# A decoder layer's expert lookup: first-table matmuls in 64-column tiles, and the one-hots built token by token on VectorE

## The chip, the cores and the metric

The kernel runs on one core of a Trainium2 chip. The metric is the device time of one execution in microseconds (us); lower is better. Kernels are compared by the median of several executions.

The engines that matter here are TensorE (PE in the profile; its weight loads are PEld), VectorE (DVE), ScalarE (ACT), GpSimd (POOL) and SyncE (SP), which starts the transfers. Each has its own instruction stream, and they meet only at semaphores.

## The reference, cut to what matters

A decoder layer in three parts: a single-head linear attention with a causal mask, a dynamic-time-warping alignment against a context, and a product-key expert layer. The change lies in the third:

```python
# x: 32*256 rows of 256; 8 heads, 8 experts of 16384 a head and row; fp32 throughout
sim = einsum('pbnhd,hkpd->pbnhk', q, keys_p)          # 2 x 64 scores a head
scores, idx = top_k(sim, 8)                           # the best 8 of each half
all_scores = scores[0][..., :, None] + scores[1][..., None, :]
sc, pk = top_k(all_scores, 8)                         # the best 8 pairs
indices = take(idx[0] * 64 + idx[1], pk)
wd = down[indices]
hmid = sigmoid(sc) * gelu(einsum('bnd,bnhkd->bnhk', inputs, wd))
out = einsum('bnhk,bnhkd->bnd', hmid, up[indices])
x = layernorm(x + out)
```

An index is at most 64*63 + 63 = 4095, so only the first 4096 rows of `down` and `up` are reached.

## The kernel before, in words

Nothing is gathered. The kernel computes all 4096 hidden values of every row with the first table (`dnT`, transposed), applies gelu, multiplies by a coefficient that is the gate where an expert was chosen and zero elsewhere, and multiplies by the second table (`up`).

The coefficients of a row are an outer product summed over its 64 picks: expert = 32 * p + c, with p (0 to 127) in `valsT[:, :, 0]`, c (0 to 31) in `valsT[:, :, 1]`, and the gate in `valsT[:, :, 2]`. The partition of these is the pick (64 picks of a row of each of the group's two tiles, 128 together), the column is the token. For each token there are two one-hots: `hot_hi` (128 picks by 128 values of p) and `hot_lo` (128 picks by 64: 32 values of c for each of the two tiles, times the gate). TensorE multiplies them, `hot_hi` as the stationary operand in two halves of 64 columns.

The third part works on 32 groups of 256 rows. A group has 16 steps (NQ = 16), each of 8 tokens (TQ = 8; a column of `valsT` serves a row of both tiles) and 2 of the 32 values of c. The order is written out by hand, and each engine runs one loop over groups: the first two and the last two groups are peeled, and a loop of two groups a pass does the rest.

- VectorE in a step q: `hots` for step q + 3 (AHEAD = 3; four buffers of one-hots, so it waits for the matmuls of step q - 1), then `coefs` of step q, which multiplies the coefficients in PSUM into `gelh`. `norm` of the group before comes in step 0, `scale` in step 6. After the 16 steps it runs `route` twice (top 8, pairs, indices) for the group two ahead.
- GpSimd in a step: one multiply of `hot_lo` by the gate, after VectorE's `hot_ready`; it signals `gated_ready`.
- TensorE in a step: `coefs` (wait for `gated_ready` and for the PSUM bank of two steps ago; 16 matmuls of 64 columns), then `hidden` of the next group (4 matmuls of 128 stationary columns and 256 moving ones; PSUM banks in turn, freed by gelu). `turn_vals` (transposes of the picks) comes in step 10, `turn` in step 15. After the steps: `score` for tile 0, half an `output` of 32 matmuls, `score` for tile 1, and the other 48 `output` matmuls.
- ScalarE: gelu of each `hidden` result, the gates' sigmoid, the copies of transposes.

In the profile each fp32 matmul is two records of TensorE: the 16 of `coefs` are 32, the 4 of `hidden` are 8.

Of the kernel before, what the change touches and what calls it, by code (L numbers as in the profile page):

```python
# [15 lines left out]
ALU = mybir.AluOpType  # L16
# [3 lines left out]
P = 128  # L20
# [5 lines left out]
def decoder_layer(nc, x, xT, ctx_rows_d, ctx_cols_d, wqkvT_d, bqkv_d, projT_d, projb_d, gamma_d, beta_d, wq_d,  # L26
# [4 lines left out]
    CC = C // P  # L31
# [14 lines left out]
    with ctx:  # L46
        def sb(name, shape, dt=F32):
            return ctx.enter_context(nc.sbuf_tensor(name, shape, dt))

        def sem(name):  # L50
            return ctx.enter_context(nc.semaphore(name))
# [12 lines left out]
        iota = sb("iota", [P, T])  # L64
# [81 lines left out]
        pool_rests, dve_rests, act_rests = sem("pool_rests"), sem("dve_rests"), sem("act_rests")  # L146
# [15 lines left out]
        gate_ready = sem("gate_ready")  # L162
        valsT_mm = sem("valsT_mm")
        valsT_ready = sem("valsT_ready")
        hot_ready = sem("hot_ready")
        gated_ready = sem("gated_ready")
        a_mm = sem("a_mm")
        coef_ready = sem("coef_ready")
# [13 lines left out]
        def rest(eng, spare):  # L182

            eng.sem_inc(spare, 1)

        def later(b, n):

            return not (isinstance(b, int) and b < n)
# [28 lines left out]
        with ExitStack() as st:  # L217
# [33 lines left out]
            block = st.enter_context(nc.Block())  # L251
# [295 lines left out]
        with ExitStack() as st:  # L547
# [32 lines left out]
            block = st.enter_context(nc.Block())  # L580
# [267 lines left out]
        with ExitStack() as st:  # L848
            def se(name, shape, dt=F32):
                return st.enter_context(nc.sbuf_tensor(name, shape, dt))  # L850
# [3 lines left out]
            NQ = 16  # L854
            TQ = P // NQ
            CL = 32
            BUFS = 4
            dnT = se("dnT", [P, CC, CL, P])
            up = se("up", [P, CL, C])
            gelh = se("gelh", [P, 2, CL, 2, P])  # L860
            hot_hi = se("hot_hi", [P, BUFS, TQ, P])
            hot_lo = se("hot_lo", [P, BUFS, TQ, 2 * CL])
            offs = se("offs", [P, 2 * CL])
            x2_res = se("x2_res", [P, 2, 2, C])
            x2T = se("x2T", [P, CC, 2, P])
# [11 lines left out]
            valsT = se("valsT", [P, 2, 3, P])  # L877
# [9 lines left out]
            ps_h = [bank[3 + i][:, :].rearrange("p (c n) -> p c n", c=2) for i in range(2)]  # L887
# [8 lines left out]
            def groups(eng, step):  # L896

                for g in range(2):
                    step(g, g)
                with eng.Fori(1, GROUPS // 2 - 1) as j:  # L900
                    for par in range(2):
                        step(2 * j + par, par)
                for g in range(GROUPS - 2, GROUPS):
                    step(g, g % 2)
# [5 lines left out]
            block = st.enter_context(nc.Block())  # L910
# [34 lines left out]
                for par in range(2):  # L945
                    sp.wait_ge(y_out[par], 16 * GROUPS // 2)

            @block.gpsimd
            def _(pool):
                def gated(g, par, q):  # L950

                    pool.wait_ge(hot_ready, g * NQ + (q + 1))
                    rest(pool, pool_rests)
                    pool.tensor_tensor(hot_lo[:, q % BUFS], hot_lo[:, q % BUFS],  # L954
                                       valsT[:, par, 2, TQ * q:TQ * (q + 1), None].to_broadcast([P, TQ, 2 * CL]),
                                       ALU.mult).then_inc(gated_ready, 1)

                def step(g, par):
                    for q in range(NQ):
                        gated(g, par, q)  # L960
                groups(pool, step)

            @block.tensor
            def _(pe):
                def turn(g, par):
# [29 lines left out]
                def hidden(g, q):  # L995

                    pe.wait_ge(x2T_ready, g + 1)
                    if later(g, 1) or q >= 2:
                        pe.wait_ge(gel_ready, g * NQ + (q - 1))
                    for c in range(2):  # L1000
                        for k in range(CC):
                            mm = pe.matmul(ps_h[q % 2][:, c, :], dnT[:, k, 2 * q + c, :],  # L1002
                                           x2T[:, k, :, :].rearrange("p a t -> p (a t)"),
                                           start=(k == 0), stop=(k == CC - 1))
                    mm.then_inc(h_mm, 1)

                def coefs(g, q):
# [24 lines left out]
                for q in range(NQ):  # L1032
# [4 lines left out]
                    for k in range(CC):  # L1037
                        for c in range(2):
                            mm = pe.transpose(ps_dn[q % 4][:, k, c, :], dn[:, 2 * q + c, k * P:(k + 1) * P], ident[:, :])
# [3 lines left out]
                for q in range(NQ):  # L1043
                    hidden(0, q)
# [101 lines left out]
            def _(dve):  # L1146
# [52 lines left out]
                def hots(g, par, q):  # L1199

                    if q == 0:
                        dve.wait_ge(valsT_ready, g + 1)
                    if later(g, 1) or q >= BUFS:
                        dve.wait_ge(a_mm, g * NQ + (q + 1 - BUFS))
                    rest(dve, dve_rests)
                    some = slice(TQ * q, TQ * (q + 1))
                    dve.tensor_tensor(hot_hi[:, q % BUFS], iota[:, None, 0:P].to_broadcast([P, TQ, P]),  # L1207
                                      valsT[:, par, 0, some, None].to_broadcast([P, TQ, P]), ALU.is_equal)
                    dve.tensor_tensor(hot_lo[:, q % BUFS], offs[:, None, :].to_broadcast([P, TQ, 2 * CL]),  # L1209
                                      valsT[:, par, 1, some, None].to_broadcast([P, TQ, 2 * CL]), ALU.is_equal)\  # L1210
                        .then_inc(hot_ready, 1)

                def coefs(g, par, q):

# [37 lines left out]
                for q in range(AHEAD):  # L1252
                    hots(0, 0, q)
# [63 lines left out]
```

## Time and profile before

| | |
|---|---|
| Median of 3 runs | 3309.46 us (3308.94 to 3311.43) |
| The profiled execution's own time | 3312.22 us |
| Its span in the profile | 3310.5 us |
| PE busy | 3016.2 us (91%), 26660 instructions |
| DVE busy | 2774.3 us (84%), 8246 instructions |
| ACT busy | 736.2 us (22%) |
| POOL busy | 597.7 us (18%), of which 536.1 in the gate multiply |

Busy time says who works, not who is waited for: the chain of waits does that. Durations of neighbouring VectorE instructions overlap by some tens of ns, so what a further instruction costs is read from the distance between two starts, called spacing below, and not from its duration alone. The third part begins at about 590 us of the span; the first one-hot is written at 620.83 us.

### The profile page before, as it was taken

What the parts mean: (1) busy time and instruction counts of PE and PEld (TensorE: products, weight loads), DVE (VectorE), ACT (ScalarE), POOL (GpSimd) and SP (SyncE); (2) the same over time, 40 slices, a digit from 0 to 9 for tenths busy, and PEclk for the clock granted to TensorE, in tenths of its full rate; (3) what the DMA queues carried; (4) which work ended last, traced back from release to release, by engine and by line L of the source; (5) the groups of instructions that cost most, each with busy time, mean ns of one, the idle gap of its engine ahead of it and who ended that gap; (6) DMA issues with size and microseconds to landing.
All of it is one profiled execution on the core that took longest, in us unless ns stands there. A gap on an engine that the chain in (4) does not pass through costs nothing.

```text
span 3310.5 us, 73159 instructions
## 1 busy us (share of the span) xinstructions
PE 3016.2 (91%) x26660; PEld 2388.6 (72%) x26660; DVE 2774.3 (84%) x8246; ACT 736.2 (22%) x1302; POOL 597.7 (18%) x599
## 2 busy tenths in 40 slices
PE   8981047699999999999999999999999999999997
PEld 4651035588888888888888888888888888888886
DVE  5557977798889898989898988888888888888865
ACT  3540024212222222222222222222222222222210
POOL 1230000022222121212122222222222222222221
PEclk9985555899999999999999999999999999999997
DMA  5441025200000000000000000000000000000000
GB/s 154 140 132 46 0 73 172 73 1 11 11 11 11 11 11 11 11 11 11 11 11 11 11 11 11 11 12 11 12 11 12 11 11 11 11 11 11 8 8 7
DMA packets 88552, 93.42 MB, mean 28 GB/s; under 512 B 6109, under 2 KB 86910, under 8 KB 88062
## 3 DMA queue, kind: packets, MB, share of 16 engines
q1 hardware_dynamic: 88206, 88.74, 8.6%
q8 instruction: 225, 3.69, 0.4%
q14 instruction: 121, 0.99, 0.1%
HBM read 60.94 MB, written 27.79 MB: 27 GB/s over the span
## 4 chain that ended last, share of the span: by engine, by line
PE 80%; DVE 2%; issue 0%; ACT 0%; DVEq 0%; ACTq 0%
PE bank L1002 29%; PE bank L1025 27%; PE bank L1015 16%; PE bank L982 7%; PE bank L973 1%; DVE hot_hi L1207 1%; PE bank L992 0%; ACT dnT L1117 0%; DVE top_i L1157 0%; DVE gelh L1220 0%; DVE hot_lo L1209 0%; DVE top L1153 0%; DVE sel_i L1171 0%; DVE sel L1167 0%; DVEq L1238 0%
## 5 line engine op out<-in xcount | busy, mean ns | idle before, releaser
L1002 PE MATMUL bank<-x2T,dnT 128*128 128x256 f32 x4096 | 1011.8, 390 | 0.4 <-ACT gelh L1104 0.4
L954 POOL TENSOR_TENSOR hot_lo<-hot_lo,valsT 128x512 f32<-128x512 f32 x512 | 536.1, 1047 | 2492.5 <-DVE hot_lo L1209 2492.5
L1207 DVE TENSOR_TENSOR hot_hi<-iota,valsT 128x1024 f32<-128x1024 f32 x512 | 858.7, 1677 | 52.2 <-issue 36.7
L1025 PE MATMUL bank<-up,gelh 128*128 128x256 f32 x4096 | 896.6, 380 | 0.9 <-DVE gelh L1220 0.9
L1025 PEld LDWEIGHTS bank<-up,gelh 128*128 128x128 f32 x4096 | 779.8, 190 | 133.1 <-issue 28.7
L1002 PEld LDWEIGHTS bank<-x2T,dnT 128*128 128x128 f32 x4096 | 738.1, 190 | 111.2 <-issue 1.3
L1015 PEld LDWEIGHTS bank<-hot_lo,hot_hi 128*64 128x64 f32 x16384 | 529.5, 140 | 195.7 <-issue 178.5
L1015 PE MATMUL bank<-hot_lo,hot_hi 128*64 128x64 f32 x16384 | 600.2, 227 | 28.2 <-DVE gelh L1220 27.6
L1104 ACT ACTIVATE gelh<-bank 128x512 f32<-128x512 f32 x512 | 305.7, 597 | 938.6 <-PE bank L1002 937.9
L1220 DVE TENSOR_TENSOR gelh<-bank,gelh 128x512 f32<-128x512 f32 x512 | 347.6, 679 | 52.4 <-PE bank L1015 49.6
L1209 DVE TENSOR_TENSOR hot_lo<-offs,valsT 128x512 f32<-128x512 f32 x512 | 349.5, 683 | 0.0
L1153 DVE MAX8 top<-bank 128x8 f32<-128x64 f32 x1024 | 140.8, 216 | 145.0 <-PE bank L982 144.8
L982 PE MATMUL bank<-keymap,xnT 128*128 128x512 f32 x512 | 237.6, 608 | 9.5 <-DVE top_i L1157 6.2
L1157 DVE FIND_INDEX8 top_i<-top,bank 128x8 uint32<-128x64 f32 x1024 | 205.1, 225 | 0.0
L982 PEld LDWEIGHTS bank<-keymap,xnT 128*128 128x128 f32 x512 | 99.6, 195 | 110.6 <-issue 103.2
L1104 ACT ACT_TABLE_LOAD x62 | 79.5, 1283 | 382.1 <-PE bank L1002 382.1
L677 PE MATMUL bank<-fold,lo_hi 128*80 128x32 f32 x4 | 0.7, 326 | 178.0 <-DVEq L780 178.0
L677 PEld LDWEIGHTS bank<-fold,lo_hi 128*80 128x80 f32 x4 | 0.6, 242 | 178.2 <-DVEq L780 178.2
L1093 ACT ACTIVATE vals<-sel 128x64 f32<-128x64 f32 x64 | 16.5, 257 | 413.0 <-DVE sel L1167 412.7
L1093 ACT ACT_TABLE_LOAD x32 | 41.1, 1283 | 298.6 <-DVE sel L1167 298.6
L1171 DVE FIND_INDEX8 sel_i<-sel,pair 128x8 uint32<-128x64 f32 x512 | 101.1, 220 | 0.0
L1179 DVE TENSOR_TENSOR pick<-half_i,iota 128x512 f32<-128x512 uint32 x128 | 82.8, 689 | 4.8
(140 smaller groups left out, 1994.2 us busy)
## 6 DMA issues: line engine op xcount, KB each, us to landing
x_scratch<-x_sb SPq DMA_DIRECT2D x64, 256.0 KB, 2.2
xT_sb<-in_xT SPq DMA_DIRECT2D x32, 256.0 KB, 2.7
x_sb<-in_x SPq DMA_DIRECT2D x32, 256.0 KB, 2.8
x_again<-x_scratch SPq DMA_DIRECT2D x32, 256.0 KB, 2.6
x_tile<-x_scratch SPq DMA_DIRECT2D x32, 256.0 KB, 3.0
x_res<-x_scratch SPq DMA_DIRECT2D x32, 256.0 KB, 2.8
out_y<-yo SPq DMA_DIRECT2D x32, 256.0 KB, 2.2
gelh<-in_table SPq DMA_DIRECT2D x4, 1024.0 KB, 8.9
```

What stands on the lines that cost most here:

```text
L954: pool.tensor_tensor(hot_lo[:, q % BUFS], hot_lo[:, q % BUFS], valsT[:, par, 2, TQ * q:TQ * (q + 1), None].to_broadcast([P, TQ, 2 * CL]), ...
L982: mm = pe.matmul(ps_score[p][:, :], xnT[:, k, a, :], keymap[:, k, p * NH * NK:(p + 1) * NH * NK], start=(k == 0), stop=(k == CC - 1))
L1002: mm = pe.matmul(ps_h[q % 2][:, c, :], dnT[:, k, 2 * q + c, :], x2T[:, k, :, :].rearrange("p a t -> p (a t)"), start=(k == 0), stop=(k == ...
L1015: mm = pe.matmul(ps_a[q % 2][rows, t * 2 * CL:(t + 1) * 2 * CL], hot_hi[:, q % BUFS, t, rows], hot_lo[:, q % BUFS, t, :], start=True, stop ...
L1025: mm = pe.matmul(ps_out[:, a, :], gelh[:, par, c, a, :], up[:, c, :], start=(c == 0), stop=(c == CL - 1))
L1104: act.activation(gelh[:, par, 2 * q:2 * q + 2, :, :].rearrange("p c a t -> p c (a t)"), ps_h[q % 2], ACT.Gelu).then_inc(gel_ready, 1)
L1153: dve.max(out=top[:, p, h, :], in_=ps_score[p][:, h * NK:(h + 1) * NK])
L1157: last = dve.max_index(out=top_i[:, p, h, :], in_max=top[:, p, h, :], in_values=ps_score[p][:, h * NK:(h + 1) * NK])
L1171: dve.max_index(out=sel_i[:, h, :], in_max=sel[:, h, :], in_values=pair[:, h, :, :].rearrange("p a b -> p (a b)"))
L1207: dve.tensor_tensor(hot_hi[:, q % BUFS], iota[:, None, 0:P].to_broadcast([P, TQ, P]), valsT[:, par, 0, some, None].to_broadcast([P, TQ, P] ...
L1209: dve.tensor_tensor(hot_lo[:, q % BUFS], offs[:, None, :].to_broadcast([P, TQ, 2 * CL]), valsT[:, par, 1, some, None].to_broadcast([P, TQ, ...
L1220: dve.tensor_tensor(some, ps_a[q % 2][:, :].rearrange("p (t a c) -> p c a t", t=TQ, a=2), some, ALU.mult)\
```

## The change

The first-table matmuls of `hidden` are split: instead of 4 matmuls of 128 stationary columns there are 8 of 64, which write the lower and the upper 64 partitions of the same PSUM tile in turn. The moving operand stays the whole 256 columns, so each is streamed twice.

The one-hots of a step are no longer two VectorE instructions over 8 tokens and one on GpSimd. They are 16 VectorE instructions, two a token, with the token's value as a per-partition scalar operand: one compares `iota` with p, the other compares `offs` with c and multiplies by the gate. GpSimd does nothing in the third part, and VectorE signals `gated_ready` itself.

```diff
@@ GpSimd
-            @block.gpsimd
-            def _(pool):
-                def gated(g, par, q):
-
-                    pool.wait_ge(hot_ready, g * NQ + (q + 1))
-                    rest(pool, pool_rests)
-                    pool.tensor_tensor(hot_lo[:, q % BUFS], hot_lo[:, q % BUFS],
-                                       valsT[:, par, 2, TQ * q:TQ * (q + 1), None].to_broadcast([P, TQ, 2 * CL]),
-                                       ALU.mult).then_inc(gated_ready, 1)
...
@@ TensorE, hidden
-                            mm = pe.matmul(ps_h[q % 2][:, c, :], dnT[:, k, 2 * q + c, :],
-                                           x2T[:, k, :, :].rearrange("p a t -> p (a t)"),
-                                           start=(k == 0), stop=(k == CC - 1))
+                            for half in range(2):
+                                rows = slice(half * P // 2, (half + 1) * P // 2)
+                                mm = pe.matmul(ps_h[q % 2][rows, c, :], dnT[:, k, 2 * q + c, rows],
+                                               x2T[:, k, :, :].rearrange("p a t -> p (a t)"),
+                                               start=(k == 0), stop=(k == CC - 1))
@@ VectorE, hots
-                    some = slice(TQ * q, TQ * (q + 1))
-                    dve.tensor_tensor(hot_hi[:, q % BUFS], iota[:, None, 0:P].to_broadcast([P, TQ, P]),
-                                      valsT[:, par, 0, some, None].to_broadcast([P, TQ, P]), ALU.is_equal)
-                    dve.tensor_tensor(hot_lo[:, q % BUFS], offs[:, None, :].to_broadcast([P, TQ, 2 * CL]),
-                                      valsT[:, par, 1, some, None].to_broadcast([P, TQ, 2 * CL]), ALU.is_equal)\
-                        .then_inc(hot_ready, 1)
+                    for t in range(TQ):
+                        at = TQ * q + t
+                        dve.tensor_scalar(hot_hi[:, q % BUFS, t, :], iota[:, 0:P], valsT[:, par, 0, at:at + 1], None,
+                                          ALU.is_equal)
+                        last = dve.tensor_scalar(hot_lo[:, q % BUFS, t, :], offs[:, :], valsT[:, par, 1, at:at + 1],
+                                                 valsT[:, par, 2, at:at + 1], ALU.is_equal, ALU.mult)
+                    last.then_inc(gated_ready, 1)
```

VectorE's stream in two steps in the middle of a group, before the change. L1207 and L1209 write the one-hots of the step three ahead, L1220 multiplies the coefficients of this step into `gelh`.

```order
959 L1207 TENSOR_TENSOR hot_hi<-iota,valsT 128x1024 [waits a_mm]
960 L1209 TENSOR_TENSOR hot_lo<-offs,valsT 128x512
961 L1217 REGISTER_ALU
962 L1220 TENSOR_TENSOR gelh<-bank,gelh 128x64x8 [waits a_mm]
963 L1207 TENSOR_TENSOR hot_hi<-iota,valsT 128x1024 [waits a_mm]
```

The same place after it, where the lines are numbered lower since the GpSimd block is gone (L1194 and L1196 are the one-hots, L1207 is the multiply):

```order
1519 L1207 TENSOR_TENSOR gelh<-bank,gelh 128x64x8 [waits a_mm]
1520 L1194 TENSOR_SCALAR hot_hi<-iota,valsT 128x128 [waits a_mm]
1521 L1196 TENSOR_SCALAR hot_lo<-offs,valsT 128x64
1522 L1194 TENSOR_SCALAR hot_hi<-iota,valsT 128x128
1523 L1196 TENSOR_SCALAR hot_lo<-offs,valsT 128x64
...
1536 L1204 REGISTER_ALU
1537 L1207 TENSOR_TENSOR gelh<-bank,gelh 128x64x8 [waits a_mm]
```

A step of VectorE has gone from three instructions to 17; the waits stand where they stood. The total number of elements written is the same.

TensorE's stream in one step, before the change. L1015 is `coefs`, L1002 is `hidden`; a row's last number is its count.

```order
501 L1015 MATMUL bank<-hot_lo,hot_hi 64x64 [waits coef_ready,gated_ready]
502 L1015 MATMUL bank<-hot_lo,hot_hi 64x64 x15
504 L1002 MATMUL bank<-x2T,dnT 128x256 [waits gel_ready]
505 L1002 MATMUL bank<-x2T,dnT 128x256 x3
507 L1015 MATMUL bank<-hot_lo,hot_hi 64x64 [waits coef_ready,gated_ready]
```

And after it (L1001 is `coefs`, L988 is `hidden`):

```order
501 L1001 MATMUL bank<-hot_lo,hot_hi 64x64 [waits coef_ready,gated_ready]
502 L1001 MATMUL bank<-hot_lo,hot_hi 64x64 x15
503 L983 REGISTER_ALU [waits x2T_ready]
504 L988 MATMUL bank<-x2T,dnT 64x256 [waits gel_ready]
505 L988 MATMUL bank<-x2T,dnT 64x256 x7
```

Nothing is reordered; every matmul of a step now has 64 stationary columns. `gated_ready` is now raised by VectorE, directly behind its last one-hot.

## Rows read from the trace of the kernel before

**Rows 1.** The page's chain that ended last, by engine and line

```profile
PE 80%; DVE 2%; issue 0%; ACT 0%; DVEq 0%; ACTq 0%
```

**Rows 2.** Chain in order of time, one group: start us, us, what

```profile
1914.14 1.08 PE bank L1015 x32
1915.22 1.92 PE bank L1002 x8
...
1936.74 1.73 PE bank L1002 x8
...
1953.89 3.43 PE bank L982 x8
...
1967.66 20.72 PE bank L1025 x96
```

**Rows 3.** Timeline of ACT, line L1099: start us, us, what

```profile
690.19 0.48 ACT L1099 ACTIVATE valsT<-bank 128x384 f32<-128x384 f32 x1
...
3188.85 0.48 ACT L1099 ACTIVATE valsT<-bank 128x384 f32<-128x384 f32 x1
```

**Rows 4.** Timeline of DVE, end of route and first steps of a group

```profile
2040.73 2.20 DVE L1153 MAX8 top<-bank 128x8 f32<-128x64 f32 x16 [3.92 <-PE bank L982]
...
2069.79 1.22 DVE L1207 TENSOR_TENSOR hot_hi<-iota,valsT 128x1024 f32<-128x1024 f32 x1
...
2073.49 0.68 DVE L1226 TENSOR_TENSOR y<-bank,x_res 128x512 f32<-128x512 f32 x1
...
2075.26 1.23 DVE L1207 TENSOR_TENSOR hot_hi<-iota,valsT 128x1024 f32<-128x1024 f32 x1
2076.41 0.68 DVE L1209 TENSOR_TENSOR hot_lo<-offs,valsT 128x512 f32<-128x512 f32 x1
2077.01 0.68 DVE L1220 TENSOR_TENSOR gelh<-bank,gelh 128x512 f32<-128x512 f32 x1
2077.61 1.78 DVE L1207 TENSOR_TENSOR hot_hi<-iota,valsT 128x1024 f32<-128x1024 f32 x1
...
2080.52 1.86 DVE L1207 TENSOR_TENSOR hot_hi<-iota,valsT 128x1024 f32<-128x1024 f32 x1
```

**Rows 5.** Timeline of DVE and POOL in mid-group

```profile
2009.72 1.04 POOL L954 TENSOR_TENSOR hot_lo<-hot_lo,valsT 128x512 f32<-128x512 f32 x1 [1.86 <-DVE hot_lo L1209]
2010.06 0.15 DVE L1237 RECIPROCAL rs<-sd 128x2 f32<-128x2 f32 x1
2010.29 0.94 DVE L1242 TENSOR_SCALAR yo<-y,mv,rs 128x256 f32<-128x256 f32 x2
2011.15 1.21 DVE L1207 TENSOR_TENSOR hot_hi<-iota,valsT 128x1024 f32<-128x1024 f32 x1
```

**Rows 6.** L516, two per-partition scalars: duration minimum/median/maximum; one pair, timeline

```profile
L516 DVE TENSOR_SCALAR x_sb<-y,mv,rs x64: 389/404/1182, 48.1 to 229.8; 128x256 f32<-128x256 f32 x64
...
201.98 0.72 DVE L516 TENSOR_SCALAR x_sb<-y,mv,rs 128x256 f32<-128x256 f32 x2
```

**Rows 7.** Groups by line and form (busy us, mean ns): copies and casts

```profile
L536 DVE CAST iota<-iota_i 128x256 f32<-128x256 int32 x1 | 0.3, 271 | 0.0
L537 DVE CAST iota<-iota_i 128x8 f32<-128x8 int32 x1 | 0.2, 152 | 0.0
```

**Rows 8.** Timeline of DVE, small instructions with an immediate or one scalar

```profile
2049.99 0.20 DVE L1175 TENSOR_SCALAR half_i<-sel_i 128x64 uint32<-128x64 uint32 x1
2050.11 0.19 DVE L1176 TENSOR_SCALAR half_i<-sel_i 128x64 uint32<-128x64 uint32 x1
...
519.63 0.48 DVE L789 SCALAR_TENSOR_TENSOR mask<-iota,bounds,ramp 77x256 f32<-77x256 f32 x1 [0.33 <-issue]
520.03 0.15 DVE L814 SCALAR_TENSOR_TENSOR nb<-mv,rs 128x2 f32<-128x2 f32 x1
```

**Rows 9.** Waits over the span: us in total, times, longest us

```profile
DVE hot_hi L1207 <- issue: 36.7, 13, 3.0
```

**Rows 10.** Windows: us, busy (x) by engine, PEclk, DMA share, GB/s

```profile
120.00:230.00 110.00, 107.27 (x514) 68.70 (x513) 62.26 (x204) 60.10 (x155) 33.74 (x39) 0.92 0.41 133
```

More of the change, by code:

```diff
@@ L164, in decoder_layer @@
         valsT_ready = sem("valsT_ready")
-        hot_ready = sem("hot_ready")
         gated_ready = sem("gated_ready")
@@ L946, in _ @@
                     sp.wait_ge(y_out[par], 16 * GROUPS // 2)
-            @block.gpsimd
-            def _(pool):
-                def gated(g, par, q):
-                    pool.wait_ge(hot_ready, g * NQ + (q + 1))
-                    rest(pool, pool_rests)
-                    pool.tensor_tensor(hot_lo[:, q % BUFS], hot_lo[:, q % BUFS],
-                                       valsT[:, par, 2, TQ * q:TQ * (q + 1), None].to_broadcast([P, TQ, 2 * CL]),
-                                       ALU.mult).then_inc(gated_ready, 1)
[L958 to L961, printed above, removed]
             @block.tensor
```

## The prediction

> **What bounds the kernel now.** I read the chain of waits first, then the timelines of single engines. The chain puts 80% of the span on TensorE [rows 1]. In order of time it is TensorE alone [rows 2]: a step is 1.08 us of coefficient matmuls (L1015) and 1.92 us of first-table matmuls (L1002), 3.0 us, with no wait. Behind the 16 steps come scores and the second table, from 1953.89 to 1988.38. The copy of `valsT` comes once a group: its first and last starts are 30 groups apart, (3188.85 - 690.19)/30 = 83.29 us a group [rows 3]. TensorE sets this period.
>
> VectorE is close behind. It starts a `hot_hi` every 2.91 us in mid-group (2077.61 to 2080.52), waits 3.92 us for the scores once a group, and otherwise hardly stops [rows 4]. So it has 0.1 us of slack a step. The question is whether its new step still fits beside TensorE's.
>
> **What VectorE gives back.** Undisturbed, `hot_hi` occupies 1.15 us (start 2075.26, next start 2076.41), `hot_lo` 0.60 and the multiply 0.60: 2.35 us. Nearly every later `hot_hi` lasts 1.78 us [rows 4], since GpSimd's multiply of 1.04 us runs beside its start. That pause goes with the GpSimd work: 2.91 would be 2.35 if nothing else changed.
>
> **What VectorE's 16 new instructions cost.** 8 tokens, each with one 128-column compare (one scalar read per partition) and one 64-column compare and multiply (two such scalars). The trace has neither, so I build them from spacing, start to start.
> - Per column: `hot_hi` against `hot_lo`, (1.15 - 0.60)/512 = 1.07 ns with two tensor inputs. A cast of 256 columns against one of 8: (271 - 152)/248 = 0.48 ns with one tensor input [rows 7]. So one-input instructions from SBUF run two columns at a time.
> - Fixed: L1175 to L1176, 64 columns and an immediate, is 0.12 us [rows 8]. Less 64 x 0.5 that is 85 ns.
> - Per-partition scalars: L516 has exactly two, over 256 columns. A pair lasts 0.72 us, one 0.404, so the second starts 0.32 us after the first [rows 6]. Less 130 for the columns and 85 fixed, two scalars cost 105 ns, some 52 each. L789, with one scalar and two tensors, is followed after 0.40 us [rows 8]; 256 x 1.07 and the 60 ns that `hot_lo` takes above its columns make 0.33, which leaves 70 ns for one scalar.
>
> Does L516 really run two columns at a time, with dear scalars, or one, with free ones? Columns at 1.07 ns would be 274 of its 320 ns, so the spacing alone allows both. The same form in L1242 decides it for me: its pair grows from 0.72 to 0.94 us when a GpSimd multiply runs beside it [rows 5], as `hot_hi` grows. The Trainium skill, "SBUF — State Buffer", says that a one-input VectorE instruction is held off by GpSimd only in a two-port mode. By that rule the 0.94 speaks for two columns at a time; no run so far shows the mode itself.
>
> So the 128-column compare is 64 + 85 + 55 = 204 ns, and the 64-column one 32 + 85 + 105 = 222 ns: 426 ns a token, 3.41 us a step. With the multiply's 0.60 the step is **4.01 us**, against 2.91 now and against TensorE's 3.0. Bounds from the nearest rows: with free scalars and columns at full price it is L516's 320 ns less 128 and less 192 columns at 1.07, 183 + 115 = 298 ns a token, giving a step of 2.98; with full price for both, 524 ns, giving 4.8. I take 426, which rests on the one form with two scalars. Break-even: VectorE's period equals 83.29 when the step is 3.14 us, or 317 ns a token.
>
> **What TensorE saves, and why it doesn't count.** Each first-table matmul becomes two on different halves of the array. A 256-column record takes 1.73/8 = 216 ns, so a 64-column one alone would take 54; the 32 of L1015 take 1.08 us, 34 ns each [rows 2], so halves do run side by side. Behind the transposes the 8 records of L1002 take 1.73 us instead of 1.92 [rows 2]: 0.19 us is lost at the switch from 64-column to 128-column matmuls. The Trainium skill, "TensorEngine Tiling (Array Packing)", section Tiling Modes, says that changing the tiling mode drains TensorE; the 0.19 agrees. With one mode throughout I expect 2.8 us a step, at most 2.6 if `coefs` gains as well. This lies under VectorE's 4.0 us and is worth nothing. The one place without one-hots, `hidden` of group 0, keeps its 1.73.
>
> **The new period.** VectorE per group: 16 x 4.01 = 64.2; two routes 2040.73 to 2069.79 = 29.06; `norm` 2073.49 to 2075.26 = 1.77 [rows 4]; `scale` 2010.06 to 2011.15 less the GpSimd pause of 0.22 = 0.87 [rows 5]. Sum 95.9. No wait is left in it. The scores of tile 0 need step 15 of TensorE, which may run as soon as VectorE has finished step 13, so they are done before the route and the 3.92 us goes. The second table takes 1953.89 + 3.43 to 1967.66 + 20.72 = 31.1 us with the score inside [rows 2], while VectorE runs routes and a set of one-hots, 29.1 + 3.4 = 32.5: just covered. VectorE's waits for code at the loop's start, 36.7 us in 13 [rows 9], were in TensorE's shadow and now count.
>
> Sum against the span of 3310.5: 30 x (95.9 - 83.29) = 378, and 37 for the loop's start. The first three sets take 10.2 us from 620.83, 2 us beyond the score that follows. Eleven steps of group 0 before the first `valsT` mark, 11 x (4.01 - 2.91) = 12. Five steps of group 30 behind the last mark, 5 x (4.01 - 3.0) = 5. In the last group 12 steps write one-hots, 12 x 1.10 = 13. Total +447, a span of 3757. The profiled execution's own time is 1.7 above its span and 2.8 above the median, so the median would be **3756 us**, 13.5% slower.
>
> **The rivals.**
> - *A, on the other side: scalars cost nothing, columns full price.* For it: L516's 0.32 us, and L1175's 0.12, fit as well. Against: L1242 beside GpSimd, and 70 ns for L789's scalar. A VectorE step of 2.98 makes its group 47.7 + 31.7 and 1.2 for the loop, 80.6; TensorE's with 0.19 saved a step is 80.25. So about 80.6, 30 x 2.7 = 81 less and some back at the ends: 3235.
> - *B, on the other side too: two columns at a time and scalars hidden behind the instruction before.* 149 + 117 = 266 ns a token, step 2.73, under TensorE's 2.81. Then TensorE stays the bound and its 0.19 a step counts: 31 x 16 x 0.19 = 94, so 3215. It decides from 276 ns a token down; between 276 and 317 VectorE sets the pace and is still faster than before. Against it: L516's pair would be spaced 215 ns and is 320. The Trainium skill, "VectorE: DVE Perf Modes", section on the TRN2 errata, gives 58 cycles and half a cycle a column here: as an estimate 127 + 94 = 221 ns a token. By that rule B holds; the trace's two-scalar row speaks against it.
> - *C: the halves do not run side by side over 256 columns.* `hidden` would take 16 x 216 = 3.45 us, a step 4.53, a group 107.8: +24.5 x 31 and 28 for group 0's `hidden`, 4100. Against it: the 34 ns.
> - *D: dearer scalars or full-price columns besides.* 474 to 524 ns a token: +48 to +98 x 4096 tokens = 200 to 400 more, 3950 to 4150.
> - *E: TensorE, idle a third of the time, is granted less clock.* At 1.2 GHz its step would be 5.6 us and set the pace. Against it: at 0.92 mean in the first part [rows 10], where it has small work with gaps. It would be busy without a pause as soon as it slowed. Some 100 us on top of the forecast if it happens in part.
>
> **How the numbers follow.** Forecast 0.70, A 0.10, B 0.05, C 0.03, D 0.08, E 0.04. Each 10 ns a token is 41 us; the forecast's own range is +-25 ns, 3655 to 3860. A range with eight chances in ten takes some of D and E and ends at 3930, and on the low side 3600. What can be told from no change is 0.2%, 7 us. Faster: A and B, 0.15. Same: a token within a few ns of 317, 0.02. Slower: the rest, 0.83.
>
> **What the profile after would show.** VectorE busy in nearly every slice, and most of the chain on the two one-hot lines; `valsT` starts 97 us apart; a token's two instructions spaced 0.43 us, the 64-column one no cheaper than the 128-column one; TensorE waiting for VectorE's `hot_lo` about 1.2 us a step; L988's 16 records in 1.7 us. I am wrong if a token takes under 317 ns, or if L988's records are spaced 216 ns.

## The result, and the profile after

The changed kernel takes **3739.29 us** (median of 4, 3735.7 to 4032.77) against 3309.52 (3308.94 to 3311.43) for the kernel before: a ratio of **1.129** [1.127, 1.132]. The forecast was 3756, slower. One of the four runs, the one of 4032.77 us, had a granted clock of 0.749 against 0.927 to 0.930 in the others; it is left out of the ratio, and no profile shows why it was slow. The profiled execution took 3740.94 us with a span of 3739.2, 428.7 longer than that of before.

The page after: busy time by engine, then VectorE in 40 slices, the chain by engine and by line, and the groups that answer to the changed lines.

```profile
PE 2999.6 (80%) x30756; PEld 2259.9 (60%) x30756; DVE 3349.2 (90%) x15414; ACT 735.7 (20%) x1302; POOL 61.5 (2%) x87
...
DVE  4557786999999999999999999999999999999975
...
DVE 57%; PE 19%; issue 6%; DVEq 3%; ACT 0%; ACTq 0%
DVE hot_lo L1196 21%; DVE hot_hi L1194 19%; PE bank L1011 14%; DVE gelh L1207 8%; DVE top_i L1143 2%; PE bank L1001 2%; PE bank L966 2%; DVE top L1139 1%; DVE sel_i L1157 1%; PE bank L988 1%; DVE sel L1153 1%; DVEq L1214 1%; DVE pick L1165 0%; DVE pick L1170 0%; DVE half_key L1173 0%
...
L1196 DVE TENSOR_SCALAR hot_lo<-offs,valsT 128x64 f32<-128x64 f32 x4096 | 1251.4, 306 | 0.0
L1194 DVE TENSOR_SCALAR hot_hi<-iota,valsT 128x128 f32<-128x128 f32 x4096 | 1132.6, 277 | 52.8 <-issue 36.9
L1001 PE MATMUL bank<-hot_lo,hot_hi 128*64 128x64 f32 x16384 | 603.7, 228 | 445.0 <-DVE gelh L1207 443.8
...
L1139 DVE MAX8 top<-bank 128x8 f32<-128x64 f32 x1024 | 140.0, 211 | 8.2 <-PE bank L966 8.2
```

The chain has turned over: 80% on TensorE [rows 1] is now 57% on VectorE, most of it on the two one-hot lines. VectorE is at 9 from the eighth slice to the last but two. TensorE's busy time is nearly unchanged, but `coefs` (L1001) now sits idle behind VectorE for 444 us. The route's wait for scores, 3.92 us in the group of [rows 4] and 144.8 us in the whole run before, is down to a single wait of 8.2 us (L1139).

VectorE's timeline after, one step of mid-group, against [rows 4]:

```profile
2047.13 0.68 DVE L1207 TENSOR_TENSOR gelh<-bank,gelh 128x512 f32<-128x512 f32 x1
2047.73 0.28 DVE L1194 TENSOR_SCALAR hot_hi<-iota,valsT 128x128 f32<-128x128 f32 x1
2047.93 0.31 DVE L1196 TENSOR_SCALAR hot_lo<-offs,valsT 128x64 f32<-128x64 f32 x1
2048.15 0.28 DVE L1194 TENSOR_SCALAR hot_hi<-iota,valsT 128x128 f32<-128x128 f32 x1
...
2051.08 0.68 DVE L1207 TENSOR_TENSOR gelh<-bank,gelh 128x512 f32<-128x512 f32 x1
```

A token is 0.42 us (2047.73 to 2048.15), a step 3.95 (2047.13 to 2051.08), with no wait in it. Note that the durations, 0.28 and 0.31, would make 0.59 a token: neighbours overlap, and only the spacing adds up.

The copies of `valsT` after, against [rows 3]; the first and last are 30 groups apart:

```profile
704.82 0.49 ACT L1085 ACTIVATE valsT<-bank 128x384 f32<-128x384 f32 x1
...
1954.41 0.48 ACT L1085 ACTIVATE valsT<-bank 128x384 f32<-128x384 f32 x1
...
2052.47 0.49 ACT L1085 ACTIVATE valsT<-bank 128x384 f32<-128x384 f32 x1
...
2147.73 0.48 ACT L1085 ACTIVATE valsT<-bank 128x384 f32<-128x384 f32 x1
...
3592.37 0.49 ACT L1085 ACTIVATE valsT<-bank 128x384 f32<-128x384 f32 x1
```

(3592.37 - 704.82)/30 = 96.25 us a group, 83.29 before. These two groups take 98.06 and 95.26 us. The loop holds two groups, and in every second one VectorE waits some 2.8 us at the loop's start (the 36.9 us of L1194, in 13 waits; the profile names nothing that it waited for). Over the run the groups with that wait take 97.05 to 98.06 us and the others about 95.2, so 1.8 to 2.8 us of it shows in the period.

TensorE after, behind the second table of one group, where finished one-hots wait for it; then the first step that VectorE holds up:

```profile
2106.77 1.15 PE L1001 MATMUL bank<-hot_lo,hot_hi 128*64 128x64 f32 x32
2107.76 1.90 PE L988 MATMUL bank<-x2T,dnT 128*64 128x256 f32 x16
2109.49 1.10 PE L1001 MATMUL bank<-hot_lo,hot_hi 128*64 128x64 f32 x32
2110.42 1.90 PE L988 MATMUL bank<-x2T,dnT 128*64 128x256 f32 x16
...
2118.61 1.15 PE L1001 MATMUL bank<-hot_lo,hot_hi 128*64 128x64 f32 x32 [0.98 <-DVE gelh L1207]
```

The 16 records of L988 take 1.73 us (2107.76 to 2109.49), 108 ns each where a whole one of 128 columns takes 216 (1.73/8 in [rows 2]): the halves run side by side. `coefs` takes 0.93 (2109.49 to 2110.42), so an unhindered step is 2.66 us, where [rows 2] had 1.08 + 1.92 = 3.0. TensorE got faster and waits.

Is it the narrower form that is faster, or that the form no longer changes? The last step of a group before the change tells. There the whole matmuls of `hidden` stand between transposes and scores, which have 128 stationary columns too:

```profile
2035.26 1.89 PE L1002 MATMUL bank<-x2T,dnT 128*128 128x256 f32 x8
2036.99 3.60 PE L982 MATMUL bank<-keymap,xnT 128*128 128x512 f32 x8
```

They take 1.73 us (2035.26 to 2036.99), just as long as the halves. So the narrow form is no faster in itself; what was saved lay at the changes between 64 and 128 columns.

### The profile page after: what moved, and what is told of

Read it like the earlier page. It is cut to its first block, busy times and chain, and to the rows that moved or that the text cites. A ratio compares the mean times of both kernels' runs of the same rounds, so it can differ in the third digit from the quotient of the medians.

```text
span 3739.2 us, 87018 instructions
## 1 busy us (share of the span) xinstructions
PE 2999.6 (80%) x30756; PEld 2259.9 (60%) x30756; DVE 3349.2 (90%) x15414; ACT 735.7 (20%) x1302; POOL 61.5 (2%) x87
## 4 chain that ended last, share of the span: by engine, by line
DVE 57%; PE 19%; issue 6%; DVEq 3%; ACT 0%; ACTq 0%
DVE hot_lo L1196 21%; DVE hot_hi L1194 19%; PE bank L1011 14%; DVE gelh L1207 8%; DVE top_i L1143 2%; PE bank L1001 2%; PE bank L966 2%; DVE top L1139 1%; DVE sel_i L1157 1%; PE bank L988 1%; DVE sel L1153 1%; DVEq L1214 1%; DVE pick L1165 0%; DVE pick L1170 0%; DVE half_key L1173 0%
## 5 line engine op out<-in xcount | busy, mean ns | idle before, releaser
L1196 DVE TENSOR_SCALAR hot_lo<-offs,valsT 128x64 f32<-128x64 f32 x4096 | 1251.4, 306 | 0.0
L1194 DVE TENSOR_SCALAR hot_hi<-iota,valsT 128x128 f32<-128x128 f32 x4096 | 1132.6, 277 | 52.8 <-issue 36.9
L988 PE MATMUL bank<-x2T,dnT 128*64 128x256 f32 x8192 | 1009.0, 388 | 0.4 <-ACT gelh L1090 0.4
L1001 PE MATMUL bank<-hot_lo,hot_hi 128*64 128x64 f32 x16384 | 603.7, 228 | 445.0 <-DVE gelh L1207 443.8
L1001 PEld LDWEIGHTS bank<-hot_lo,hot_hi 128*64 128x64 f32 x16384 | 558.1, 142 | 629.7 <-DVE hot_lo L1196 596.2
L988 PEld LDWEIGHTS bank<-x2T,dnT 128*64 128x64 f32 x8192 | 630.3, 140 | 184.9 <-issue 12.5
L1207 DVE TENSOR_TENSOR gelh<-bank,gelh 128x512 f32<-128x512 f32 x512 | 348.3, 680 | 40.3 <-issue 29.8
L1139 DVE MAX8 top<-bank 128x8 f32<-128x64 f32 x1024 | 140.0, 211 | 8.2 <-PE bank L966 8.2
L1170 DVE TENSOR_TENSOR pick<-pick,top_i 128x512 f32<-128x512 f32 x128 | 82.8, 688 | 4.8
```

The lines of the kernel that those rows point to most:

```text
L988: mm = pe.matmul(ps_h[q % 2][rows, c, :], dnT[:, k, 2 * q + c, rows], x2T[:, k, :, :].rearrange("p a t -> p (a t)"), start=(k == 0), stop= ...
L1001: mm = pe.matmul(ps_a[q % 2][rows, t * 2 * CL:(t + 1) * 2 * CL], hot_hi[:, q % BUFS, t, rows], hot_lo[:, q % BUFS, t, :], start=True, stop ...
L1139: dve.max(out=top[:, p, h, :], in_=ps_score[p][:, h * NK:(h + 1) * NK])
L1194: dve.tensor_scalar(hot_hi[:, q % BUFS, t, :], iota[:, 0:P], valsT[:, par, 0, at:at + 1], None, ALU.is_equal)
L1196: last = dve.tensor_scalar(hot_lo[:, q % BUFS, t, :], offs[:, :], valsT[:, par, 1, at:at + 1], valsT[:, par, 2, at:at + 1], ALU.is_equal, ...
L1207: dve.tensor_tensor(some, ps_a[q % 2][:, :].rearrange("p (t a c) -> p c a t", t=TQ, a=2), some, ALU.mult)\
```

## The experiments

Theory T: VectorE sets the pace by the one-hots of its 4096 tokens, and a token costs about 75 fixed ns for each of its two instructions, 0.5 ns a column and some 55 ns for each per-partition scalar. Rivals: one column at a time with cheap scalars; instruction count alone; the halves on TensorE; the clock. In each experiment the mean group is the distance over 30 groups between two `valsT` copies, those that stand at 704.82 and 3592.37 above; they are called marks.

### halves_only

The kernel before, with the first-table halves alone:

```diff
-                            mm = pe.matmul(ps_h[q % 2][:, c, :], dnT[:, k, 2 * q + c, :],
+                            for half in range(2):
+                                rows = slice(half * P // 2, (half + 1) * P // 2)
+                                mm = pe.matmul(ps_h[q % 2][rows, c, :], dnT[:, k, 2 * q + c, rows],
```

> The first-table matmuls in 64-column halves, one-hots as before (two VectorE instructions a step and GpSimd's gate multiply). My theory: in the changed kernel a TensorE step that waits for nothing takes 2.66 us against 3.0 before, so TensorE alone would need 83.29 - 16 x 0.34 = 77.9 us a group. VectorE, with its step of 2.91 us beside GpSimd, needs 16 x 2.91 + 31.9 + 1.3 for the loop's start = 79.8, so it becomes the bound: about 30 x 3.5 = 105 us less than before and some more at the ends, 3190 to 3215 us, with valsT starts 79.8 us apart. Rival 1: the halves gain nothing by themselves (TensorE's step of 2.66 came only from its weights being ready early, because VectorE was late): 3309. Rival 2: TensorE is still the bound at 77.9 us: 3150.

Measured: 3226.39 us (3225.88 to 3233.51), ratio 0.975 [0.973, 0.977]. The marks:

```profile
688.03 0.49 ACT L1101 ACTIVATE valsT<-bank 128x384 f32<-128x384 f32 x1
...
3102.06 0.48 ACT L1101 ACTIVATE valsT<-bank 128x384 f32<-128x384 f32 x1
```

80.47 us a group, 2.82 less than before, and 30 x 2.82 = 85 is the whole gain. The expectation is missed by 11 us at its upper end. VectorE is now the slower in the steps, as expected:

```profile
2039.06 1.78 DVE L1209 TENSOR_TENSOR hot_hi<-iota,valsT 128x1024 f32<-128x1024 f32 x1
2040.76 0.68 DVE L1211 TENSOR_TENSOR hot_lo<-offs,valsT 128x512 f32<-128x512 f32 x1
...
2041.97 1.78 DVE L1209 TENSOR_TENSOR hot_hi<-iota,valsT 128x1024 f32<-128x1024 f32 x1
```

That is 2.91 us a step, against TensorE's 2.66. But VectorE doesn't set the whole group, as the expectation had it. It still waits for the scores:

```profile
DVE top L1155 <- PE bank L982: 60.9, 32, 8.2
```

One of the 32 waits is the 8.2; the others are 1.7 us each. The expectation had no such wait; it had 79.8 us a group, and 80.47 were measured. So the halves are a gain by themselves; what the one-hots cost is the next run's question.

### onehots_only

The changed kernel, with the first-table matmuls whole again:

```diff
-                            for half in range(2):
-                                rows = slice(half * P // 2, (half + 1) * P // 2)
-                                mm = pe.matmul(ps_h[q % 2][rows, c, :], dnT[:, k, 2 * q + c, rows],
+                            mm = pe.matmul(ps_h[q % 2][:, c, :], dnT[:, k, 2 * q + c, :],
```

> The token-wise one-hots of the changed kernel with the first-table matmuls as before (128 columns). My theory: VectorE sets the pace with 3.95 us a step and TensorE's 3.0 fits under it, so the halves are worth nothing there: 3739, within 0.3%. The end of a group could show a little: TensorE's second table with the score inside takes 31.1 us against VectorE's 32.4 us of route and one-hots. Rival: the halves were worth their 0.34 us a step in the changed kernel too, and it would be 3739 + 16 x 32 x 0.34 = 3913 without them.

Measured: 3733.72 us (3730.08 to 3736.67), ratio 1.128 [1.125, 1.130], which overlaps the full change's interval, as expected. TensorE still has time to spare in a step, 0.74 us in the first one after a second table that VectorE holds up and 0.87 in those after it:

```profile
2010.25 1.99 PE L986 MATMUL bank<-x2T,dnT 128*128 128x256 f32 x8
2012.99 1.15 PE L999 MATMUL bank<-hot_lo,hot_hi 128*64 128x64 f32 x32 [0.74 <-DVE gelh L1205]
```

The one-hots cost 422 us against the 3311.26 of before on the same chip, and under them the halves' 85 are worth nothing. The two parts do not add: 422 less 85 would be 337, and the full change costs 430.

### immediates

The changed kernel with constants in place of the three per-partition scalars; its one-hots are not those of the picks.

```diff
-                        dve.tensor_scalar(hot_hi[:, q % BUFS, t, :], iota[:, 0:P], valsT[:, par, 0, at:at + 1], None,
+                        dve.tensor_scalar(hot_hi[:, q % BUFS, t, :], iota[:, 0:P], 5.0, None,
...
-                        last = dve.tensor_scalar(hot_lo[:, q % BUFS, t, :], offs[:, :], valsT[:, par, 1, at:at + 1],
-                                                 valsT[:, par, 2, at:at + 1], ALU.is_equal, ALU.mult)
+                        last = dve.tensor_scalar(hot_lo[:, q % BUFS, t, :], offs[:, :], 3.0,
+                                                 0.5, ALU.is_equal, ALU.mult)
```

> The changed kernel with constants (5.0; 3.0 and 0.5) in place of the three per-partition scalars of a token; the one-hots are then not those of the picks. Same instructions, columns and waits. My theory: each per-partition scalar costs 50 to 55 ns, so a token falls from 418 to about 260 ns, VectorE's step from 3.95 to 2.70 us, and TensorE (77.9 us a group) and VectorE (76.4) are nearly even: about 78 us a group, 3150 to 3180 us. Rival: the scalars are free and the columns are at full price; a token stays at 418 ns and the time at 3739.

Measured: 3168.38 us (one run). Same number of instructions, same columns, and 571 us less. VectorE's timeline:

```profile
2009.58 0.21 DVE L1194 TENSOR_SCALAR hot_hi<-iota 128x128 f32<-128x128 f32 x1
2009.71 0.18 DVE L1196 TENSOR_SCALAR hot_lo<-offs 128x64 f32<-128x64 f32 x1
...
2011.47 0.67 DVE L1207 TENSOR_TENSOR gelh<-bank,gelh 128x512 f32<-128x512 f32 x1
```

Its eighth token ends at 2011.47, its first began at 2009.58: 1.89 us, 236 ns a token instead of 420. The three scalars cost 184 ns, 61 each. Instruction count and columns together are 236 ns. With them VectorE's step is 2.49 us, under TensorE's 2.66, so TensorE sets the pace here; the 571 us are what the scalars cost down to that floor, not all of VectorE's saving. The Trainium skill, "VectorE: DVE Perf Modes", section on the TRN2 errata, gives 221 ns for these two forms, as an estimate; without scalars it comes within 15 ns, and with them it is 200 short.

### half_columns

The changed kernel with `hot_hi` written in 64 of its 128 columns and zeroed once ahead in the rest; experts with p over 63 get no coefficient.

```diff
-                        dve.tensor_scalar(hot_hi[:, q % BUFS, t, :], iota[:, 0:P], valsT[:, par, 0, at:at + 1], None,
+                        dve.tensor_scalar(hot_hi[:, q % BUFS, t, 0:P // 2], iota[:, 0:P // 2], valsT[:, par, 0, at:at + 1], None,
```

> The changed kernel with the 128-column compare writing only 64 of its 128 columns (the rest stays zero from one fill ahead of the groups, some 4 us), so half of hot_hi is left out. My theory, two columns at a time: 64 columns are worth 33 ns a token, 418 to 385 ns, the step 3.69, 3739 - 31.5 x 16 x 0.26 = about 3610 us. Rival, one column at a time: 67 ns a token, step 3.41, about 3470 us. Rival, a floor that goes by instruction and not by columns: 3740.

Measured: 3606.8 us (one run). First and last mark:

```profile
694.20 0.48 ACT L1085 ACTIVATE valsT<-bank 128x384 f32<-128x384 f32 x1
...
3466.02 0.48 ACT L1085 ACTIVATE valsT<-bank 128x384 f32<-128x384 f32 x1
```

92.39 us a group, so 64 columns are (96.25 - 92.39)/128 = 30 ns, 0.47 ns a column. At the 1.07 ns of the two-tensor `hot_hi` it would have been 68 ns and about 3470 us. So this instruction, with its scalar, goes through its columns twice as fast as `hot_hi` before did: two columns at a time, in the prediction's words.

### one_scalar

The changed kernel with the gate left out of `hot_lo`, so that L1196 reads one scalar instead of two; coefficients are 1 where an expert was chosen.

```diff
                         last = dve.tensor_scalar(hot_lo[:, q % BUFS, t, :], offs[:, :], valsT[:, par, 1, at:at + 1],
-                                                 valsT[:, par, 2, at:at + 1], ALU.is_equal, ALU.mult)
+                                                 None, ALU.is_equal)
```

> The changed kernel with only one per-partition scalar in the 64-column instruction (the compare; the gate is left out). My theory, each scalar costs 52 ns by itself: a token 418 to 366 ns, a step 3.95 to 3.53, about 3530 us. Rival, the first scalar of an instruction costs and the second is free: 3739.

Measured: 3511.71 us (one run).

```profile
698.89 0.49 ACT L1085 ACTIVATE valsT<-bank 128x384 f32<-128x384 f32 x1
...
3373.02 0.48 ACT L1085 ACTIVATE valsT<-bank 128x384 f32<-128x384 f32 x1
```

89.14 us a group: the second scalar costs (96.25 - 89.14)/128 = 56 ns. It isn't hidden behind the first. This edit takes out the multiply along with its scalar, so by itself it could be the price of the second operation. The immediates run rules that out: it kept the multiply, with a constant, and there `hot_lo` was followed after 0.10 us (2009.71 to 2009.81 in its timeline) instead of 0.22. It is the operand that costs. With that the term that decided the sign is settled.

### no_gate

halves_only with the gate left out and GpSimd idle; coefficients are 1 where an expert was chosen. What the old one-hots cost without the GpSimd multiply beside them:

```diff
-                    pool.tensor_tensor(hot_lo[:, q % BUFS], hot_lo[:, q % BUFS],
-                                       valsT[:, par, 2, TQ * q:TQ * (q + 1), None].to_broadcast([P, TQ, 2 * CL]),
-                                       ALU.mult).then_inc(gated_ready, 1)
...
-                        .then_inc(hot_ready, 1)
+                        .then_inc(gated_ready, 1)
```

> The halves, the two-instruction one-hots of before, and no gate multiply at all (the gate is left out of the result); GpSimd is idle. My theory: hot_hi lasts 1.2 us every time, VectorE's step is 2.35 us, TensorE's 2.66 sets a group of 77.9 us: 3140 to 3150 us. Rival: hot_hi stays at 1.78 us since it wasn't GpSimd that stretched it, and the time at halves_only's 3226.

Measured: 3163.37 us (one run). VectorE's timeline:

```profile
2011.70 1.22 DVE L1193 TENSOR_TENSOR hot_hi<-iota,valsT 128x1024 f32<-128x1024 f32 x1
2012.83 0.68 DVE L1195 TENSOR_TENSOR hot_lo<-offs,valsT 128x512 f32<-128x512 f32 x1
...
2014.43 0.73 DVE L1228 TENSOR_SCALAR yo<-y,mv,rs 128x256 f32<-128x256 f32 x2
```

`hot_hi` is 1.22 us throughout instead of 1.78, and the pair that was 0.94 in [rows 5] is 0.73. So it is GpSimd's multiply that stretches both, as the prediction read it. The group is 78.78 us, that of immediates 78.81: this is TensorE's own period. The expectation, 77.9 from 2.66 us a step, is missed by 0.9 us a group. The rest lies around the transposes, which still have 128 columns. The step with `turn_vals` takes 3.29 us in this run (2022.97 to 2026.26) as in the kernel before (2018.37 to 2021.66), so it gains nothing; the last step takes 3.49 against 3.31, and the scores behind it 3.54 against 3.43.

### gate_on_vector

halves_only with the gate as a third VectorE instruction over 8 tokens, GpSimd idle:

```diff
+                    dve.drain()
+                    dve.tensor_tensor(hot_lo[:, q % BUFS], hot_lo[:, q % BUFS],
+                                      valsT[:, par, 2, some, None].to_broadcast([P, TQ, 2 * CL]),
+                                      ALU.mult).then_inc(gated_ready, 1)
```

> The halves, and the gate multiply as a third VectorE instruction over the 8 tokens (hot_lo, hot_hi, then a drain and the multiply). GpSimd is idle. My theory: VectorE's step is 1.15 + 0.60 + 0.60 + 0.60 and some 0.08 for the drain, 3.03 us, against 2.91 with GpSimd's help: 16 x 3.03 + 33.2 = 81.7 us a group, 3226 + 30 x 1.8 = about 3280 us. Rival: the drain costs more, 0.3 us a step: 85 us a group, 3390.

Measured: 3350.93 us (3349.22 to 3356.2), ratio 1.012 [1.011, 1.014], about 1% slower than the kernel before. It lies between the theory's 3280, missed by 71 us, and the rival's 3390. VectorE's timeline:

```profile
2054.76 0.68 DVE L1193 TENSOR_TENSOR hot_lo<-offs,valsT 128x512 f32<-128x512 f32 x1
2055.36 1.22 DVE L1195 TENSOR_TENSOR hot_hi<-iota,valsT 128x1024 f32<-128x1024 f32 x1
2056.66 0.69 DVE L1198 TENSOR_TENSOR hot_lo<-hot_lo,valsT 128x512 f32<-128x512 f32 x1
2057.26 0.68 DVE L1209 TENSOR_TENSOR gelh<-bank,gelh 128x512 f32<-128x512 f32 x1
```

0.60 + 1.30 + 0.60 + 0.60 = 3.10 us a step, 0.15 of it at the drain behind `hot_hi` (0.08 expected), over TensorE's 2.66. That is 16 x 0.07 = 1.1 us of the 2.6 by which a group missed the 81.7; the rest was not taken apart. Without GpSimd VectorE does the one-hots in 3 wide instructions in a step of 3.1 us, where with the 16 narrow ones the step is 3.95; both include the multiply into `gelh`. The change would have lost less this way, and still lost.

### gate_on_scalar

halves_only with the gate as 8 ScalarE activations a step, one a token, set ahead of the step's gelu:

```diff
+                    for t in range(TQ):
+                        at = TQ * q + t
+                        last = act.activation(hot_lo[:, q % BUFS, t, :], hot_lo[:, q % BUFS, t, :], ACT.Copy,
+                                              scale=valsT[:, par, 2, at:at + 1])
+                    last.then_inc(gated_ready, 1)
```

> The halves, the two-instruction one-hots of before on VectorE, and the gate multiply neither on GpSimd nor on VectorE but on ScalarE, which is idle 80% of the time: 8 activations a step (a copy of 64 columns with the gate as a per-partition scale, in place). My theory: without GpSimd beside it VectorE's step falls from 2.91 to 2.35 us, TensorE's 2.66 is the bound, and a group takes 77.9 us. ScalarE must stay under 2.66 too: two activations of 256 columns with two per-partition operands are spaced 0.46 us, so 0.25 to 0.30 for 64 columns, 2.0 to 2.4 us a step, and 0.5 for gelu: 2.5 to 2.9. About 3145 us if it fits, up to 3225 if ScalarE sets the pace at 2.9. Rival: ScalarE's order (a gate set ahead of each gelu) delays gelu and with it TensorE's PSUM banks, worse than before the change: over 3310.

Measured: 3259.77 us (3258.89 to 3260.73), ratio 0.984 [0.983, 0.986]; missed, slower than expected (3145, at most 3225), though not over 3310 as the rival had it. ScalarE's timeline and TensorE's waits:

```profile
2012.08 2.02 ACT L1099 ACTIVATE hot_lo<-hot_lo,valsT 128x64 f32<-128x64 f32 x8 [0.16 <-DVE hot_lo L1211]
...
2014.00 0.58 ACT L1091 ACTIVATE gelh<-bank 128x512 f32<-128x512 f32 x1
```

```profile
PE bank L989 <- ACT gelh L1091: 53.1, 43, 2.0
```

Eight gates and a gelu fill 2.5 of a step's 2.66 us, and a gelu behind the gates comes late for the PSUM bank that `hidden` waits for. These waits are 53 of the 96 us by which this run is longer than no_gate.

### gate_behind_gelu

gate_on_scalar with the gates moved behind the step's gelu:

```diff
-                        if q + 3 < NQ:
-                            gated(g, par, q + 3)
...
                             gelu(g + 1, 1 - par, q)
+                        if q + 3 < NQ:
+                            gated(g, par, q + 3)
```

> As gate_on_scalar (all 8 gate activations on ScalarE), but each step's gates behind its gelu instead of ahead. In gate_on_scalar TensorE waited 53 us in all for gelu, in the first steps of a group, and 1.8 to 2.4 us a group were lost against no_gate's 78.8. My theory: gelu no longer queues behind gates, so that wait goes: 3175 to 3200 us. Rival: ScalarE's backlog at a group's start (three table loads of 1.28 us and 8 gates a step at 2.4 of 2.66 us) is what costs, whatever the order: 3260 as before, TensorE then waiting for hot_lo instead of gelu.

Measured: 3197.45 us (3194.55 to 3205.38), ratio 0.967 [0.965, 0.968]. TensorE's waits for ScalarE:

```profile
PEld bank L1002 <- ACT hot_lo L1099: 17.5, 36, 1.3
...
PE bank L989 <- ACT gelh L1091: 13.3, 31, 0.5
```

That is within the 3175 to 3200 expected. The order alone gave about 60 us back, and the wait for gelu fell from 53.1 to 13.3. 34 us over no_gate remain; the waits for ScalarE above are 31 of them if they do not overlap, which was not checked.

### gate_split

halves_only with the gate of tokens 0 to 3 on ScalarE behind gelu, and that of 4 to 7 on GpSimd:

```diff
-                    pool.tensor_tensor(hot_lo[:, q % BUFS], hot_lo[:, q % BUFS],
...
+                    pool.tensor_tensor(hot_lo[:, q % BUFS, TQ // 2:TQ], hot_lo[:, q % BUFS, TQ // 2:TQ],
...
+                    pe.wait_ge(gated_too, g * NQ + (q + 1))
...
+                    for t in range(TQ // 2):
+                        at = TQ * q + t
+                        last = act.activation(hot_lo[:, q % BUFS, t, :], hot_lo[:, q % BUFS, t, :], ACT.Copy,
+                                              scale=valsT[:, par, 2, at:at + 1])
```

> The halves, the two-instruction one-hots of before, and the gate multiply shared: tokens 0 to 3 of a step on ScalarE (4 activations), tokens 4 to 7 on GpSimd (one multiply of 256 columns). ScalarE does its share behind gelu. My theory: GpSimd's work and with it the stretch of hot_hi halves (0.56 to about 0.28 us), so VectorE's step is 2.35 + 0.28 = 2.63, ScalarE's 4 x 0.24 + 0.5 = 1.5, and TensorE's 2.66 is the bound, as without a gate: 78.8 us a group, 3163 to 3180 us. Rival: GpSimd's multiply of 256 columns is not half as long, or stretches hot_hi as much as before: VectorE at 2.91 a step and halves_only's 3226.

Measured: **3166.51 us** (3160.07 to 3171.4, 5 runs), ratio 0.957 [0.955, 0.958], the fastest complete version, faster than both kernels. Its chain, and its timeline in a step:

```profile
PE 79%; DVE 2%; issue 0%; DMA 0%; DVEq 0%; ACT 0%; SPq 0%; ACTq 0%
```

```profile
2033.43 0.61 POOL L955 TENSOR_TENSOR hot_lo<-hot_lo,valsT 128x256 f32<-128x256 f32 x1 [2.05 <-DVE hot_lo L1228]
2033.49 0.69 DVE L1239 TENSOR_TENSOR gelh<-bank,gelh 128x512 f32<-128x512 f32 x1 [0.23 <-PE bank L1019]
2034.10 1.22 DVE L1226 TENSOR_TENSOR hot_hi<-iota,valsT 128x1024 f32<-128x1024 f32 x1
...
2035.69 1.05 ACT L1116 ACTIVATE hot_lo<-hot_lo,valsT 128x64 f32<-128x64 f32 x4
...
2036.76 1.22 DVE L1226 TENSOR_TENSOR hot_hi<-iota,valsT 128x1024 f32<-128x1024 f32 x1
```

The time is as expected, but not quite for the reason given: the expectation had the stretch of `hot_hi` halved, and it is gone. GpSimd's 0.61 us now ends before `hot_hi` starts (2034.04 against 2034.10), and the multiply into `gelh` beside it isn't stretched: it takes 0.69 us, as it does without GpSimd. VectorE waits 0.23 us for TensorE and keeps to its 2.66 us. The group is 78.79, TensorE's own period: the halves' gain is collected in full.

## Why the prediction was right, point by point

- **VectorE becomes the bound**: right. Chain and slices show it, and onehots_only shows that TensorE's side no longer matters.
- **A token at 426 ns**: measured 420. The parts are less exact than the sum, and that the sum is so close is partly luck. Predicted 85 fixed, 52 a scalar and 0.5 a column. Measured: 56 (one_scalar) to 61 (immediates) a scalar, 0.47 a column (half_columns), and so (236 - 192 x 0.47)/2 = 73 fixed. The fixed part was 12 too dear twice, the scalars some 8 too cheap three times; two errors of 24 ns cancelled. What carried the sign was the choice for two columns at a time with dear scalars. half_columns confirms the columns, immediates and one_scalar the scalars. The prediction took the choice from L1242's growth beside GpSimd; no_gate shows that GpSimd was the cause of that growth, not that two columns at a time were. (The prediction's upper bound of 524 ns a token is a slip: with its own terms full-price columns make 192 x 1.07 + 170 + 160 = 535. Nothing hangs on it.)
- **A group at 95.9, and 37 us for loop starts beside**: measured 95.26 in the group without a loop start. The waits there are 36.9 us in 13, as in [rows 9], and over the 30 groups between the marks they add 30 x (96.25 - 95.26) = 30 us. Together the groups cost 389 us, against 378 + 37 predicted.
- **The ends**: ahead of the first mark 704.82 - 690.19 = 14.6 (predicted 2 + 12), behind the last (3739.2 - 3592.37) - (3310.5 - 3188.85) = 25.2 (predicted 5 + 13). Together 389 + 14.6 + 25.2 = 428.7, against 447.
- **TensorE's step at 2.8, or 2.6 if `coefs` gains as well**: 2.66. The 0.19 of `hidden` went as predicted, and `coefs` gained 0.15 besides. The Trainium skill, "TensorEngine Tiling (Array Packing)", Tiling Modes, says that a change of mode drains TensorE. The 0.34 us a step agree with it, though no row shows the drain itself.
- **TensorE waiting 1.2 us a step for `hot_lo`**: it waits 0.98 us in the step shown, and for another thing. The row names `gelh` (L1207). The profile puts 596 us of the weight loads' waits down to `hot_lo`, but the order of the streams speaks against that: VectorE writes the one-hots three steps ahead, so they are done before the multiply that frees the PSUM bank of two steps ago, and that multiply comes last. This changes nothing in the time, since both stand in VectorE's step.
- **The scores' wait goes, and the second table is just covered**: right. One wait of 8.2 us at the route is left in the run.
- **Rival A** (3235) and **B** (3215) fell with the scalars. B would have been right without them: immediates takes 3168. The VectorE step that B needed is within reach, only the operands aren't free. **C** fell with 108 ns a record. **D** would have needed 474 ns. **E**: in the profiled execution TensorE kept its clock though it waited 0.98 of 3.95 us in the step above, as a window of the profile after shows (us; busy by engine in the order PE, PEld, DVE, ACT, POOL; granted clock 0.99; DMA share; GB/s):

```profile
1700.00:2500.00 800.00, 690.75 (x7594) 529.17 (x7593) 768.15 (x3718) 141.80 (x220) 0.00 (x0) 0.99 0.03 10
```

## What to carry to other kernels

Price a VectorE instruction from spacings in the same trace, by its operands: here a per-partition scalar cost as much as 120 to 130 columns, and with constants in place of three of them (which this kernel can't use) the time fell by 571 us. When two engines are within 0.1 us of each other in a step, relieving one and loading the other is two experiments, and should be run as two: the good half of this change was invisible behind the bad one. When a helper engine slows its neighbour through shared access, halving its piece may be enough, and removing it at any price is not needed.

## What was not expected of the hardware

- **The change of form costs more than `hidden` shows.** The prediction had read 0.19 us off `hidden`. `coefs` paid too, 0.15 us (1.08 against 0.93 us). A step has two changes, from 64 to 128 columns and back, and the pair cost 0.34 us. How much falls to which direction these rows don't tell.
- **GpSimd's interference depends on when it runs.** Its 1.04 us multiply stretches `hot_hi` from 1.22 to 1.78 us, by 0.56; the 0.61 us one of gate_split, which ends ahead of `hot_hi`, leaves it at 1.22 there. The Trainium skill, "SBUF — State Buffer", describes the shared ports as an exclusive lock held for the whole instruction. In [rows 4] the `hot_hi` at 2077.61 starts while a GpSimd multiply of 1.04 us has 0.70 us to run (it starts at 2077.27), and is stretched by 0.56, somewhat less than if it had been held for all of that time. The profile's times of GpSimd are rough, and I can't tell from them whether the instruction was held at its start or throughout. Nor does every instruction suffer: the multiply into `gelh`, with one input from PSUM, takes 0.68 to 0.69 us beside GpSimd and without it.
- **ScalarE's small activations are no cheaper than VectorE's.** 8 of 64 columns with one per-partition scale took 2.02 us, 0.25 each. VectorE's token-wise compares are spaced 0.20 to 0.22. Moving the gates there paid off because ScalarE had the time: it was busy 22% of the span.
